# Gate and up by Strassen's seven products in a one-core chain of four conditioned layers

## The reference

```
x = x + w0[a]^T x + bias[a]            # 64x64 per sample, over positions
gate = x Wg + (x Ag[a]) Bg[a]          # 512 -> 2048, ranks of 16
up   = x Wu + (x Au[a]) Bu[a]
h    = silu(gate) * up
x = x + h Wd + (h Ad[a]) Bd[a]         # 2048 -> 512
x = x + x W2^T + s[b] (x A2[b]^T) B2[b]^T
x = x + w3[c]^T x                      # 64x64 per sample
```

## Time and profile before

| | before |
|---|---|
| median of 3 runs | 802.61 us (799.77 to 803.45) |
| span of the profiled execution, first to last instruction | 798.9 us |
| its own time | not listed apart; the lowest of the three runs is 799.77 |
| PE busy | 762.9 us (95%), 3820 matmuls |
| DVE, ACT, POOL busy | 388.7, 292.8, 228.1 us |
| moved by DMA | 90.65 MB, mean 113 GB/s |
| mean granted clock of TensorE | 0.991 |

### The profile page before, as it was taken

How to read it: one execution, slowest core, us unless ns; L and a number is a source line. 1 busy time by engine, 2 the same in 40 slices (tenths; PEclk the granted TensorE clock), 3 DMA queues, 4 the chain that set the end, 5 groups by cost and what they waited for, 6 DMA issues and landing times. The chain is left out here.

```text
span 798.9 us, 12005 instructions
## 1 busy us (share of the span) xinstructions
PE 762.9 (95%) x3820; PEld 643.5 (81%) x3820; DVE 388.7 (49%) x669; ACT 292.8 (37%) x552; POOL 228.1 (29%) x465
## 2 busy tenths in 40 slices
PE   3799969999899999999999999999999999999997
PEld 2688868888788888888888888888888878878885
DVE  6565424333565444444565444445444344346665
ACT  3444223333434343333344433343334343323332
POOL 5356652343312433433232433222233000000000
PEclk9899989999999999999999999999999999999999
DMA  7944433346324433433333343442343432212212
GB/s 167 202 143 135 147 93 106 107 133 212 91 72 133 121 107 107 134 107 107 111 110 120 103 129 115 134 158 66 105 132 106 103 82 79 92 54 80 106 53 79
DMA packets 123856, 90.65 MB, mean 113 GB/s; under 512 B 37168, under 2 KB 102704, under 8 KB 123824
## 3 DMA queue, kind: packets, MB, share of 16 engines
q1 hardware_dynamic: 109984, 68.75, 28.6%
q0 software_dynamic: 7808, 19.93, 8.8%
q10 hardware_dynamic: 6032, 1.58, 0.9%
HBM read 77.65 MB, written 4.19 MB: 102 GB/s over the span
## 5 line engine op out<-in xcount | busy, mean ns | idle before, releaser
L974 PE MATMUL bank<-XT,gu 128*128 128x512 f32 (+1 forms) x1536 | 377.7, 395 | 9.4 <-DVE gu L149 4.1
L974 PEld LDWEIGHTS bank<-XT,gu 128*128 128x128 f32 x1536 | 283.3, 189 | 67.0 <-issue 9.5
L1017 PE MATMUL bank<-wds,hs 128*128 128x512 f32 x768 | 187.3, 392 | 0.0
L149 DVE TENSOR_TENSOR gu<-stage,gu 128x1024 fp32r<-128x1024 f32 x64 | 78.5, 1227 | 188.2 <-ACT gu L145 187.8
L1017 PEld LDWEIGHTS bank<-wds,hs 128*128 128x128 f32 x768 | 139.8, 188 | 27.7
L138 ACT ACTIVATE gu<-stage 128x1024 fp32r<-128x1024 f32 x64 | 67.8, 1059 | 161.2 <-DMA stage<-in_L_cond_Wd_dram 157.7
L388 POOL DMA_INDIRECT braw<-in_L_cond_Bg_dram,boffs x64 | 70.9, 1107 | 172.9 <-DVE gu L149 150.9
L543 ACT ACTIVATE hs<-hid 128x512 fp32r<-128x512 f32 x64 | 40.5, 632 | 153.7 <-DVE hid L797 143.2
L404 POOL COPY adsel<-ad_raw 128x32 f32 x256 | 42.5, 213 | 178.5 <-DVE wds L791 165.3
L979 PEld LDWEIGHTS bank<-UT,gu 128*128 128x128 f32 x512 | 78.1, 189 | 9.9
L979 PE MATMUL bank<-UT,gu 128*128 128x256 f32 (+1 forms) x512 | 81.0, 281 | 0.0
(11 more groups left out here) (109 smaller groups left out, 543.3 us busy)
## 6 DMA issues: line engine op xcount, KB each, us to landing
stage<-in_L_cond_Wg_dram SPq DMA_DIRECT2D x64, 256.0 KB
stage<-in_L_cond_Wu_dram SPq DMA_DIRECT2D x64, 256.0 KB
stage<-in_L_cond_Wd_dram SPq DMA_DIRECT2D x64, 256.0 KB
xh<-X SPq DMA_DIRECT2D x8, 512.0 KB, 3.7
out_dram<-y SPq DMA_DIRECT2D x16, 256.0 KB, 2.0
X<-x1s SPq DMA_DIRECT2D x14, 256.0 KB
X<-in_x_dram SPq DMA_DIRECT2D x3, 1024.0 KB
X<-in_x_dram SPq DMA_DIRECT2D x4, 256.0 KB
```

What stands on the lines that cost most here:

```text
L149: return nc.vector.tensor_tensor(gu[s][:, 1, at, :], src, gu[s][:, 0, at, :].bitcast(f32), ALU.subtract)
L974: nc.tensor.matmul(psum[:, :], gu[s][:, a, KT * j + k, :], XT[:, b, k, ds(c, TOK)], start=(k == 0 and n == 0), stop=False)
L1017: last = nc.tensor.matmul(psD[j][:, :], hs[s][:, a, j * P:(j + 1) * P], wds[s][:, b, :], start=(first and n == 0), stop=False)
```

## The change

Gate and up are now computed on 2x2 blocks. The tokens run in two halves (`HALVES`) of 1024, the hidden features in 8 units of 256 for each half, the input features in two blocks of 256. Per unit and weight there are seven `product`s of 6 matmuls of 128x512 (Strassen's scheme in Winograd's form) for what were eight blocks. Their operands are blocks and sums of blocks: `combine` makes S1 to S4 of the weights, `xc_rest` T1 to T4 of x, seven pieces of each are split into high and low (`w_low`, `xc_low`). The products go to three banks (`psA`, `psB`, `psC`), and DVE makes the four result blocks by six additions per window (`sum_u2` to `sum_c12`); ACT copies the first product out (`p1_copy`).

A window is the gate or the up of one unit. The down product of the unit before is spread over both windows (`downs`, at 0 to 3): two `down` of 6 matmuls each, into two banks, and 4 of 128x256 for ranks. It isn't added up in PSUM any more: DVE adds each of its 8 results to X1 in SBUF (`evict`), for each unit.

Ag and Au of all adapters are laid side by side and go through the seven products as one more weight at the head of each half; `pick` then takes each sample's ranks by matmuls with a one-hot matrix (`SEL`). The x of the pairs 8 to 15 goes through layer 0 inside unit 0; its buffers (`xin`, `RD`) are shared with others, so that `load_d(0)`, the first load of Wd, waits for the last of these transposes. `lora_down` is taken out of the groups and put among the duos of layers 2 and 3: `lora_down(d + 1, q)` writes one bank, and `x2_sum` clears it. All loops are written out. Every wd, gate and up weight is loaded twice in place of four times; x1 and x2 of a half are parked in HBM.

```diff
-                def half(j, s, c, psum, done, ks=range(KT + 1)):
-
-                    for k in ks:
-                        if k < KT:
-                            for n, (a, b) in enumerate(((0, 0), (0, 1), (1, 0))):
-                                nc.tensor.matmul(psum[:, :], gu[s][:, a, KT * j + k, :], XT[:, b, k, ds(c, TOK)],
-                                                 start=(k == 0 and n == 0), stop=False)
-                            continue
-                        for q in range(DQ):
-                            for a in range(2):
-                                last = nc.tensor.matmul(psum[:, q * DTOK:(q + 1) * DTOK],
-                                                        gu[s][:, a, 2 * KT + DQ * j + q, :],
-                                                        UT[:, j, ds(c + q * DTOK, DTOK)],
-                                                        start=False, stop=(q == DQ - 1 and a == 1))
...
+                def product(psum, t, left, right, first):
+                    for k in range(2):
+                        for n, (a, b) in enumerate(THREE):
+                            last = nc.tensor.matmul(psum[:, :], WC[:, t, left, a, k, :], XC[:, right, b, k, :],
+                                                    start=(first and k == 0 and n == 0), stop=(k == 1 and n == 2),
+                                                    skip_group_check=not first)
+                    return last
+
+                def lora(psum, f, j, tok, first):
+                    for q in range(2):
+                        for a in range(2):
+                            last = nc.tensor.matmul(psum[:, q * QT:(q + 1) * QT], BL[:, a, 2 * tok + q, f * P:(f + 1) * P],
+                                                    UT[:, j, (2 * tok + q) * QT:(2 * tok + q + 1) * QT],
+                                                    start=(first and q == 0 and a == 0), stop=(q == 1 and a == 1),
+                                                    skip_group_check=True)
+                    return last
...
+                def first_products(n, t):
+                    if n:
+                        pe.wait_ge(s_add, 6 * (n - 1) + 4)
+                    product(psA, t, A11, B11, True).then_inc(s_prod, 1)
+                    if n:
+                        pe.wait_ge(s_add, 6 * (n - 1) + 5)
+                    product(psB, t, S2, T2, True).then_inc(s_prod, 1)
+                    if n:
+                        pe.wait_ge(s_add, 6 * (n - 1) + 6)
...
+                def c11_product(n, t, b):
+                    pe.wait_ge(s_p1, n + 1)
+                    product(psA, t, A12, B21, False)
+                    pe.wait_ge(s_bl, 2 * b + 1)
+                    lora(psA, 0, t, 0, False).then_inc(s_prod, 1)
+                    pe.wait_ge(s_add, 6 * n + 1)
+                    product(psB, t, S3, T3, False).then_inc(s_prod, 1)
+
+                def c21_product(n, t, b, order):
+                    pe.wait_ge(s_bl, 2 * b + 2)
+                    if t == G:
+                        pe.wait_ge(s_silu, order)
+                    else:
+                        pe.wait_ge(s_hid, order)
+                    lora(psA, 1, t, 1, True).then_inc(s_prod, 1)
+                    pe.wait_ge(s_add, 6 * n + 2)
+                    product(psB, t, A22, T4, False)
+                    lora(psB, 1, t, 0, False).then_inc(s_prod, 1)
+
+                def c12_product(n, t):
+                    pe.wait_ge(s_add, 6 * n + 3)
+                    product(psC, t, S4, B22, False)
+                    lora(psC, 0, t, 1, False).then_inc(s_prod, 1)
+
...
+                def downs(unit, at):
+                    if unit % UNITS == 0 and at == 0:
+                        ranks_start(unit // UNITS)
+                    down(unit, 2 * at)
+                    down(unit, 2 * at + 1)
+                    ranks(unit, at)
...
+                def xc_rest(h):
+                    n = 7 * h
+                    dve.wait_ge(s_xcl, n + 2)
+                    dve.wait_ge(s_xr, HP * (h + 1))
+                    nc.vector.tensor_tensor(XB11, XB12, XB11, ALU.subtract).then_inc(s_xt, 1)
+                    nc.vector.tensor_tensor(XB12, XB22, XB12, ALU.subtract).then_inc(s_xt, 1)
+                    xc_low(n + 2, B22)
+                    dve.wait_ge(s_xt, 4 * h + 2)
+                    dve.wait_ge(s_xcl, n + 3)
+                    nc.vector.tensor_tensor(XB22, XB22, XB11, ALU.subtract).then_inc(s_xt, 1)
+                    xc_low(n + 3, T1)
+                    dve.wait_ge(s_xt, 4 * h + 3)
+                    nc.vector.tensor_tensor(XB21, XB21, XB22, ALU.subtract).then_inc(s_xt, 1)
+                    for m, slot in enumerate((T2, T3, T4)):
+                        xc_low(n + 4 + m, slot)
...
+                def combine(t, w, ready):
+                    dve.wait_ge(ready[0], ready[1])
+                    a11, a12 = RW[:, t, 0:2, 0:P], RW[:, t, 2:4, 0:P]
+                    a21, a22 = RW[:, t, 0:2, P:QT], RW[:, t, 2:4, P:QT]
+                    s1, s2, s3, s4 = (SC[:, k, :].rearrange("p (k f) -> p k f", k=2) for k in range(4))
+                    nc.vector.tensor_tensor(s1, a21, a22, ALU.add).then_inc(s_comb[t], 1)
+                    nc.vector.tensor_tensor(s3, a11, a21, ALU.subtract)
+                    dve.wait_ge(s_comb[t], 3 * w + 1)
+                    nc.vector.tensor_tensor(s2, s1, a11, ALU.subtract).then_inc(s_comb[t], 1)
+                    dve.wait_ge(s_comb[t], 3 * w + 2)
+                    nc.vector.tensor_tensor(s4, a12, s2, ALU.subtract).then_inc(s_comb[t], 1)
...
+                def sum_u2(n):
+                    dve.wait_ge(s_p1, n + 1)
+                    dve.wait_ge(s_prod, 8 * n + 2)
+                    nc.vector.tensor_tensor(tmp[:, 1, :], psB[:, :], tmp[:, 0, :], ALU.add).then_inc(s_add, 1)
...
+                def evict(unit, j):
+                    g = HP * unit + j
+                    dve.wait_ge(s_down, g + 1)
+                    if unit == UNITS:
+                        dve.wait_ge(s_x1back, 16 * HP)
+                    if unit % UNITS:
+                        dve.wait_ge(s_evict, g + 1 - HP)
+                    nc.vector.tensor_tensor(X1[:, j, :], psD[j % 2][:, :], X1[:, j, :], ALU.add).then_inc(s_evict, 1)
...
+                def gate_window(h, i):
+                    n, unit = nG(h, i), UNITS * h + i
...
+                    if i == 0:
+                        for q in range(HQ):
+                            u_own(h, q)
+                    p_combine(h, i)
+                    sum_u2(n)
+                    if i:
+                        wd_low(unit - 1)
+                        hs_low(unit - 1, 0, 1, 4)
+                    b_low(2 * unit, 1)
+                    w_low(U, wP(h, i))
+                    if i:
+                        ad_low(unit - 1)
+                    if unit == 0:
...
+                def tail(h):
+                    n, unit = nP(h, UNITS - 1), UNITS * h + UNITS - 1
+                    sum_c12(n, tmp[:, 1, :])
+                    gated(unit, n, 1, 4, 4)
+                    wd_low(unit)
+                    hs_low(unit, 0, 1, 4)
+                    ad_low(unit)
+                    for j in range(HP):
+                        evict(unit, j)
+                    ud_mask(h)
...
+                def x2_sum(d, q):
+                    dve.wait_ge(s_lb, 2 * d + q + 1)
+                    if d < DUOS // 2:
+                        dve.wait_ge(s_x2in[d], 16)
+                    else:
+                        dve.wait_ge(s_evict, HP * ALL)
+                    nc.vector.tensor_tensor(x2_of(d, q), psE[:, :], x2_of(d, q), ALU.add).then_inc(s_x2, 1)
...
+                for d in range(2, DUOS):
+                    if d + 1 < DUOS:
+                        lora_down(d + 1, 0)
+                    transposes2(d)
+                    if d + 1 < DUOS:
+                        lora_down(d + 1, 1)
...
+                def load_d(unit):
+                    if unit:
+                        sp.wait_ge(s_wdl, unit)
+                    else:
+                        sp.wait_ge(s_tr, PAIRS)
+                            sp.wait_ge(s_x1st[s], 16 * HP // 2)
+                    i = unit % UNITS
+                    sp.dma_start(RD[:, :, :],
+                                 wd[i * QT:(i + 1) * QT, :].rearrange("(f p) o -> p f o", p=P)).then_inc(s_dld, 16)
```

2059 lines of the change are left out of this document (1094 added, 965 removed).

## The result

The changed kernel took 884.27 us (median of 4 runs, 882.89 to 885.37), the kernel before 803.03 us (4 runs): a ratio of 1.103, with a 95% interval of 1.100 to 1.107. The profiled execution has a span of 883.6 us. The prediction said 833 us and a range of 812 to 866: slower, as it came, but 51 us short of the measured time.

The account below looks back on a forecast made before the run. PE bounds the units, DVE the stretches around them: 36 us of PE work saved, 66 more lost, 30 longer than 799. The stretches sum to 829.1 us; medians lie 3.7 above the span, so 833 us, range 812 to 866.

Parts of the forecast that it names:

- The units: Steady gate and up windows: PE sets the pace, 35.9 us a unit, with VectorE's sums and evictions covered.
- the uncovered units: Rival: VectorE later in every window than walked, past a 1.4 us margin; 850 or 878 us, chance 12%.
- the clock in the units: Rival: one cold stretch of 2.6 us per unit, 36 us in all, 869 us; chance 3%.
- 8.15, 12.0, 6.5 and 2.7 us: Start to turn: first to second product (8.2 predicted), to fifth (12.2), before half 1 (6.6), for Wd (2.75).
- Here DVE's list stands alone, and I add it up.: Start, units 0 and 1, half's turn and end: VectorE's passes summed to place PE's waits; 66 us more lost.
- `down` can start at 120.7, a gap of 6.1: Unit 1: Wd's first load waits for the last transposes at 114.6, then load 3.7, ACT 1.06, DVE 1.23.
- the 1.75 us a pair: Start: pairs pass DVE every 1.75 us, the eighth begun at 23.5; first product at 32.4.
- the five waits: End: in five duos the second lora_down waits for an x2_sum behind both x3_low, 2.1 us each.
- the loads were rightly on the path: Unit 0: pair p + 2 is loaded only when pair p is summed, which adds 9.5 us.
- The step up to the first gate: Start: from the second product through the fifth, which waits for sum_u2 until 52.8, to the gate at 60.0 us.
- a wait of 3.2 us before stands at a granted clock of 1.00: Clock rule for the units: PE's short waits leave the clock alone; one of 6.3 us is followed by 0.5.

Follow-up runs that it names:

- e7: Changed kernel plus unread VectorE passes of 1.23 us, one in each window of units 2 to 4, two in those of units 5 to 7: 887.0 us.
- e1: Changed kernel with the 16 gathers of layer 3's rows spread two to a unit over half 1 instead of together between the halves: 865.4 us.
- e2: Changed kernel with GpSimd's gather_b(2) ahead of select_ad(0) for unit 0, the burst of 16 gathers kept: 881.7 us.
- e10: Changed kernel with the 16 gathers still in a row, but behind unit 8's adapters and rows: 879.1 us.
- e11: Changed kernel with the 16 gathers still in a row, but behind unit 12's gathers: 881.2 us.
- e3: Changed kernel with Wd's first block loaded into udp, the input buffer of the pairs, instead of RD: 877.8 us.
- e3a: Changed kernel with only xr_copy(15) moved ahead of wd_high(0) on ScalarE, Wd's load left where it was: 873.5 us.
- e8: Changed kernel with ScalarE copying pair p-3's transposes behind x_high(p) instead of pair p-2's, in the first eight pairs: 880.1 us.
- e4: Changed kernel with x2_sum(d+1, 0) ahead of x3_low(d-2) on VectorE in the loop over the duos: 873.1 us.
- e9: Changed kernel with five input buffers instead of two for pairs 8 to 15, three of them in ad_raw: 878.8 us.
- e12: Changed kernel with eight of the 16 gathers issued behind unit 12's and eight behind unit 14's: 858.2 us.
- e13: Changed kernel with the 16 gathers spread two to a unit over half 1, plus 16 unread GpSimd copies in unit 4: 860.0 us.

## Why the prediction was wrong

*Right.* The units: bound by TensorE, 35.9 us, no cold stretch (PEclk 1.00). The Trainium skill's rule on cycling banks (TensorE: Matmul & The Clock Gate, "A second HAM failure mode: psum-queue depth-cycling"), by which the clock could oscillate in the units, does not bite there: PEclk is 1.00 in all steady windows. Two rivals fall with it, the uncovered units (e7) and the clock in the units. Right too is that VectorE is alone on the path between the first products and at the turn, and how long: 8.15, 12.0, 6.5 and 2.7 us. (Less well placed: VectorE's busy time, put near 600 us, is 638.9, and TensorE's, put near 730, is 769.1.)

*The step that failed* is the one that begins with the words "Here DVE's list stands alone, and I add it up." In each stretch around the units I walked VectorE's list and took ScalarE, GpSimd and SyncE as ready. They have lists too. Of the 54.5 us that are missing, 2.3 are in the turn up to unit 8's up window and the rest here:

- *Unit 8's up window and unit 9 (18.0 us):* 16 gathers on GpSimd had no term. They cost 16 to 20 us, in two ways, each of them enough: what is behind them in GpSimd's order (e1, and the rows of e2), and VectorE and ScalarE standing while they are out (e10, e11). The first could have been read from the code and the pace of the gathers, one each 1.25 us; the second not.
- *Unit 1 (some 8 us):* "`down` can start at 120.7, a gap of 6.1" left out `xr_copy(15)`, which TensorE wants first and which stands behind `wd_high` on ScalarE. 9.0 us in place of 6.1 (e3, e3a), and cold behind it as predicted.
- *To the first product (7.9 us):* the 1.75 us a pair of the earlier trace rows was that of four pairs with another order behind it; here the eight pairs' layer 0 begins at 12.9 us for the first and 32.8 for the last, 2.8 us a pair. Some 4 us are ScalarE's order (e8), the rest about the size of the wait without a producer.
- *The end (8.3 us):* the five waits were named and sized (2.0 for 2.1), but the five duos took 73.9 us together (782.35 to 856.24) for 70.0, since matmuls at half clock behind two of these waits, some 3.5 us by e4, had no term. The other 4.4 us are before the first duo is through and were not tried apart.
- *Unit 0 (some 10 us):* e9 shows that the loads were rightly on the path. Of the 18.1 us that the stretch from the first product to unit 2 missed, unit 1 has some 8 (52.8 us from its gate to unit 2 for 45.0) and unit 0 some 10; the whole stretch varies by 6 between traces of the same code there. What else unit 0 lost was not tried alone. (The step up to the first gate also adds up to 59.1 by its own terms, not to 60.0.)

A second step was wrong beside it: "a wait of 3.2 us before stands at a granted clock of 1.00", taken as a bound below which a wait does no harm. The prediction's own has 12 matmuls in 5.46 us behind a wait of 3.12. In unit 0 of the changed kernel 12 matmuls behind a wait of 2.25 us run at a mean granted clock of 0.62:

```profile
102.87 4.60 PE L1244 MATMUL bank<-XC,WC 128*128 128x512 f32 x12 [2.25 <-DVE hid L905]
```

The same 12 in e12, behind 1.15 us, run at 1.00:

```profile
95.44 3.02 PE L1244 MATMUL bank<-XC,WC 128*128 128x512 f32 x12 [1.15 <-DVE hid L905]
```

So neither length is a bound by itself. There are two such places, in unit 0 and unit 1; their matmuls take 3.2 us less in e12, and the waits ahead of them 1.9 less, of the 6 us by which e12 is faster up to unit 1's up window.

Why VectorE and ScalarE stand during a burst is open. That copies on GpSimd don't do it (e13) and 12 indirect DMAs in a row don't in the steady part (e12) is shown; by what path 20 do is not. Waiting for their own instructions would fit e11, whose DMA records have one transfer of instructions inside the wait (it lands at 642.1 us, the wait ends at 642.81), but those of e10, which may lack some, have none from 477 to 511 us, where both of its waits lie.

## What to carry over

When a change lengthens one engine's list, walk the list of every engine that feeds it through the same stretch, GpSimd's and SyncE's too, and ask of each wait what stands in front of it; here VectorE's list alone gave two thirds of TensorE's lost time (116 of 170 us). Spread gathers that nobody needs soon over the units that have room; 16 in a row behind a unit's own four cost 17 us, two at a time nothing. And when TensorE is cold beside long waits, first see who is busy there: warming it gave 4 us at most of the 55 that were missing, while in the duos, where TensorE sets the pace, taking the waits out gave 3.5 us more than their length.
